# First three bands interleaved, first step without conv3, VectorE's order changed in the last steps

## The chip, the cores and the metric

The kernel runs on one core of one Trainium2 chip. The metric is the device time of one execution in microseconds (us), as the median over several executions. The core's engines run side by side and meet only at semaphores: TensorE (PE, its weight loads PEld), VectorE (DVE), ScalarE (ACT), GpSimd (POOL) and SyncE (SP), which issues the DMAs.

## The reference

For an image batch x of 8 x 128 x 128 positions with 64 channels, in float32:

```
q = x @ Q_P;  k, v = (3x3 neighbourhood of x) @ K_P, V_P
alpha = softmax(k . q * mask)           # over the 9 neighbours
t = x + sum(alpha * v)
u = relu(conv3x3(t, ff1) + b1)          # 64 -> 64    conv1
w = relu(conv3x3(u, ff2) + b2)          # 64 -> 128   conv2
out = t + relu(conv3x3(w, ff3) + b3)    # 128 -> 64   conv3
```

## The kernel before

The eight images are taken as four pairs; one image of a pair lies on partitions 0 to 63 (LOWER), the other on 64 to 127 (UPPER). An image is cut into 16 bands of 8 rows, so there are 64 bands. The bands run through the convolutions in one pipeline of steps, one band a step, with one draining step at the end of all.

**Attention of a band b.** `r_product` (L396) multiplies the band's x (tiles `xc` and `xs`) with `qk` = Q K^T; ACT copies the result to `rq` (`keep_r`). `masks` and `scores` (L409, L416) give the scores of patches of 8 x 8 positions against their 100 keys, in two halves; DVE takes the maxima (`max_scores`), ACT the exponentials (`exps`, 16 of them in four groups), DVE divides (`scale`). `turn` (L428) transposes the weights on PE and ACT copies them to `probt` (`keep_turned`). `mix` (L436) multiplies them with the keys' x (tile `xk`), ACT copies to `y` (`keep_y`), `v_product` (L447) multiplies with V, and DVE adds x (`add_x`, tile `xr`), which gives t in `tf`. `t_inputs` makes the inputs of conv1 (`dt`) of it. The attention of band b+2 is spread over the step of band b.

**The convolutions** are computed in Winograd form over the columns, each with four streams of products. DVE forms the inputs (`transform`, L879: part 0 the two middle streams, part 1 the two outer ones) and combines the results (`middle`, `outer`); ACT copies one bank (`keep_m2`, `keep_u2`) and applies bias and relu. Conv1 is `wholes` and `quarters` (L468, L477), conv3 four tiles of `conv3_tile` (L484), conv2 `begin2`, `go_on2`, `end2` (L532 to L564) for four tiles j. Conv3 of a step works on what conv2 of the step before left, so in the first step of all it has nothing real to work on, and its result is not stored. Conv3's first tile waits for `middle1` of the first image, its third for `outer1` and part 1 of the inputs.

**Before the first step** the attention of bands 0, 1 and 2 runs one after the other (L580 to L604 on PE, L795 on ACT, L986 on DVE): PE does all that belongs to a band before the next band begins. DVE prepares the weights of conv1 after the attention of band 0 and those of conv2 (`split_weights`) after that of band 1; GpSimd prepares those of conv3. SP issues nine small constants first, then the loads of band 0 and the weights; bands 1 and 2 are loaded into the same tiles as band 0 once its scores are done. PE waits for all weights before the first step.

**The steps.** `schedule` (L204) runs `step` on each engine: one first step, then per pair a first, fourteen middle and a last one. The last four steps of the last pair have the kinds ASK (all of the attention), MIX (only the rest from `mix` on), V (only from `v_product` on) and 0 (none); a draining step and four last tiles of conv3 follow. Each engine follows the order written out in its own `step`. DVE's (L1002) begins with `outer` of conv2 of the step before, `add_x`, `inputs` ODD part 0, ODD part 1, EVEN part 0, and `middle1` of both images.

Of the kernel before, what the change touches and what calls it, by code (L numbers as in the profile page):

```python
# [15 lines left out]
BAND = 8  # L16
# [15 lines left out]
FINAL = RUN + 1  # L32
DRAIN, LAST = BANDS, BANDS + 1
# [46 lines left out]
def build(nc, x_bands, x_keys, qt2, kt, vbd, w1, w2, w3, b1, b2, b3, window, eye, eye16, out):  # L80
    with ExitStack() as ctx:
# [27 lines left out]
        xk = sb("xk", [KEYS, PATCHES, 128], F32)  # L109
        xr = sb("xr", [128, RP, 2, W], F32)  # L110
# [22 lines left out]
        deven = sb("deven", [128, RP + 1, 4, 2, WT], F32)  # L133
        d_new = {CONV1: du, ODD: dodd[:, 2:RP + 2], EVEN: deven[:, 1:RP + 1]}
# [13 lines left out]
        r_banks = conv_banks[:, 2:4]  # L148
# [12 lines left out]
        w_ready = sem("w_ready")  # L161
# [6 lines left out]
        xr_in = sem("xr_in")  # L168
        r_done = [sem(f"r{i}_done") for i in range(2)]
# [79 lines left out]
        def split_weights(engine, wait, raw, wh, wl, mid, half, stage):  # L249
# [7 lines left out]
            engine.tensor_scalar(g2, g2, -1.0, None, ALU.mult).then_inc(stage, 1)  # L257
            wait(stage, 3)
            streams = ((0, g0), (1, mid[:, 0]), (2, mid[:, 1]), (3, g2))
            for m, g in streams:  # L260
                last = engine.tensor_copy(wh[:, m], g)
            last.then_inc(stage, 1)
            wait(stage, 4)
            for m, g in streams:
                last = engine.tensor_tensor(wl[:, m], g, wh[:, m].bitcast(F32), ALU.subtract)
# [14 lines left out]
        def _(sp):  # L280
            for dst, src in ((qt_sb, qt2), (kt_sb, kt), (v_sb, vbd), (window_sb, window), (eye_sb, eye),
                             (eye16_sb, eye16)):
                sp.dma_start(dst[:], src).then_inc(const_in, 16)
            for i, src in enumerate((b1, b2, b3)):
                sp.dma_start(bias[:, i:i + 1], src).then_inc(const_in, 16)

            def load_xc(b):
                sp.dma_start(xc[:], x_bands[b]).then_inc(xc_in, 16)

            def load_xs(b):  # L290
# [3 lines left out]
            def load_xk(b):  # L294
                sp.dma_start(xk[:], x_keys[b]).then_inc(xk_in, 16)
# [35 lines left out]
            keep_first(1, 0)  # L331
            sp.wait_ge(scores_done, 24)
            load_xs(3)
            load_xc(3)
# [14 lines left out]
            def step(G, p, k, b, par, att):  # L349
                if att >= V:  # L350
                    sp.wait_ge(t_ready, b * 2 + 2)
# [33 lines left out]
            sp.wait_ge(xk_in, 16 * LOADS)  # L385
            sp.wait_ge(xs_in, 32 * LOADS)
            sp.wait_ge(xr_in, 64 * LOADS)
            sp.wait_ge(xc_in, 16 * LOADS)

        @block.tensor  # L390
        def _(pe):
            def await_r(b):
                pe.wait_ge(xc_in, b * 16 + 16)
                pe.wait_ge(xs_in, b * 32 + 32)

            def r_product(b):  # L396
# [19 lines left out]
            def scores(b, half):  # L416
# [19 lines left out]
            def mix(b, half):  # L436
                if half == 0:
                    pe.wait_ge(xk_in, b * 16 + 16)
                pe.wait_ge(probt_ready, b * 2 + (half + 1))
                for a in range(HALF):  # L440
                    patch = half * HALF + a
                    for i, image in enumerate((LOWER, UPPER)):
                        last = nc.tensor.matmul(far_banks[image, half, a * C:(a + 1) * C], xk[:, patch, image],  # L443
# [3 lines left out]
            def v_product(b):  # L447
                moving = y[:].rearrange("c a (r s) -> c a r s", s=PATCH)
                for odd in range(2):
                    for i, image in ((1, UPPER), (0, LOWER)):  # L450
                        to = UPPER if odd != i else LOWER
                        bank = near_banks[to, i].rearrange("c (a r s) -> c a r s", r=RP, s=PATCH)
# [79 lines left out]
            def begin2(G, k, j, b, att):  # L532
# [7 lines left out]
                elif j == 2:  # L540
                    if att == ASK:
                        pe.wait_ge(probt_ready, b * 2 + 6)
                    elif att:
                        pe.wait_ge(t_ready, b * 2 + 2)
# [30 lines left out]
            pe.wait_ge(const_in, 16 * 9)  # L575
# [4 lines left out]
            for b in range(3):  # L580
                if b:
                    await_r(b)
                    pe.wait_ge(r_ready, b * 2)
# [563 lines left out]
```

## Time and profile before

| what | value |
| --- | --- |
| median of 3 executions | 2083.73 us (2083.67 to 2085.44) |
| profiled execution | 2084.2 us |
| its span in the profile | 2082.4 us |
| PE, DVE, ACT, POOL busy | 97%, 87%, 52%, 1% of the span |
| mean granted clock of PE | 0.992 |
| DMA | 320.89 MB, mean 154 GB/s |

The span is what the profiler saw from the first to the last instruction; the profiled execution took 1.8 us more than it. The granted clock is a share of PE's full 2.4 GHz: 1.00 or, when it is halved, 0.50; a stretch that holds both shows a value between. Matmul ends are modelled, so an overlap of a row with the next is no contradiction.

### The profile page before, as it was taken

The numbers are of one execution on the slowest core, as the hardware profiler recorded it, in microseconds if no ns is written. First come the engines' busy times: TensorE is split into PE (matmuls) and PEld (weight loads), VectorE is DVE, ScalarE is ACT, GpSimd is POOL, SyncE is SP. The second block draws the span as 40 slices with busy tenths as digits, with TensorE's granted clock in tenths as the row PEclk, the third lists the DMA queues.
The fourth block names the chain that finished last, engine by engine and source line by source line (L and its number), as shares of the span: only waits on it lengthen the run. The fifth ranks groups of instructions, "written<-read, shape, count | busy, mean of one in ns | idle before, by whom it ended". The sixth has DMA issues, their size and how long they took to land.

```text
span 2082.4 us, 61988 instructions
## 1 busy us (share of the span) xinstructions
PE 2025.3 (97%) x23866; PEld 1240.9 (60%) x23866; DVE 1815.4 (87%) x2502; ACT 1088.4 (52%) x3086; POOL 17.2 (1%) x28
## 2 busy tenths in 40 slices
PE   4899999999999999999999999999999999999997
PEld 3566656656665655655656655665656665665554
DVE  3699899899899899899889899899888989989986
ACT  3464555555555555555555455455455455455422
POOL 3000000000000000000000000000000000000000
PEclk9899999999999999999999999999999999999999
DMA  5555555555555555555555554554555555554532
GB/s 146 124 149 170 164 143 171 156 148 167 155 152 167 155 157 158 157 163 150 160 158 155 161 168 141 165 167 140 166 165 141 170 162 144 168 166 144 155 128 86
DMA packets 286054, 320.89 MB, mean 154 GB/s; under 512 B 87802, under 2 KB 220218, under 8 KB 279482
## 3 DMA queue, kind: packets, MB, share of 16 engines
q1 hardware_dynamic: 285982, 319.92, 53.0%
q8 instruction: 46, 0.75, 0.2%
q14 instruction: 26, 0.21, 0.0%
HBM read 150.23 MB, written 33.82 MB: 88 GB/s over the span
## 4 chain that ended last, share of the span: by engine, by line
PE 96%; DVE 2%; ACT 1%; issue 1%; DMA 0%; SPq 0%; DVEq 0%; ACTq 0%
PE conv_banks L502 32%; PE conv_banks L462 16%; PE conv_banks L527 13%; PE side_banks L527 13%; PE side_banks L443 6%; PE side_banks L422 4%; PE conv_banks L402 4%; PE side_banks L431 3%; PE side_banks L453 3%; PE side_banks L414 2%; ACT prob L724 1%; DMA xs<-x_bands 0%; DVE work L962 0%; DVE deven L882 0%; DVE deven L883 0%
## 5 line engine op out<-in xcount | busy, mean ns | idle before, releaser
L502 PE MATMUL conv_banks<-dodd,w3f 128*64 128x512 f32 (+2 forms) x1616 | 491.4, 581 | 11.0 <-DVE work L929 9.3
L502 PE MATMUL conv_banks<-deven,w3f 128*64 128x512 f32 (+2 forms) x1616 | 490.3, 579 | 0.0
L724 ACT ACTIVATE prob<-side_banks,negmax 128x100 f32<-128x100 f32 x1024 | 344.9, 378 | 162.5 <-DVE negmax L847 162.5
L462 PE MATMUL conv_banks<-dt,w1f 128*64 128x256 f32 (+2 forms) x4128 | 377.6, 378 | 0.0
L462 PEld LDWEIGHTS conv_banks<-dt,w1f 128*64 128x64 f32 (+1 forms) x4128 | 233.7, 135 | 121.0 <-issue 42.1
L502 PEld LDWEIGHTS conv_banks<-dodd,w3f 128*64 128x64 f32 x1616 | 148.3, 137 | 245.4 <-issue 219.7
L724 ACT ACTIVATION_READ_ACCUMULATOR prob<-side_banks,negmax 128x1 f32 x1024 | 246.9, 241 | 0.0
L502 PEld LDWEIGHTS conv_banks<-deven,w3f 128*64 128x64 f32 x1616 | 152.8, 137 | 143.1 <-issue 139.7
L736 ACT COPY rq<-conv_banks 128x512 f32<-128x512 f32 x128 | 68.7, 589 | 305.2 <-PE conv_banks L402 305.2
L962 DVE TENSOR_TENSOR work<-side_banks,work 128x1024 f32<-128x1024 f32 (+1 forms) x130 | 154.4, 1230 | 78.6 <-PE side_banks L527 78.6
L741 ACT COPY probt<-side_banks 100x1024 f32<-100x1024 f32 x128 | 130.2, 1017 | 157.2 <-PE side_banks L431 157.2
L527 PE MATMUL conv_banks<-duh,w2h 64*128 64x512 f32 (+2 forms) x788 | 166.6, 415 | 0.6 <-DVE work L953 0.6
L762 ACT COPY m_sb<-conv_banks 128x512 f32<-128x512 f32 x196 | 109.4, 593 | 104.6 <-PE conv_banks L527 100.3
L527 PE MATMUL side_banks<-duh,w2h 64*128 64x512 f32 (+2 forms) x788 | 157.6, 390 | 0.0
L901 DVE TENSOR_TENSOR dul<-work,duh 128x1024 fp32r<-128x1024 f32 (+1 forms) x130 | 156.7, 1205 | 0.0
L527 PE MATMUL side_banks<-duh,w2l 64*128 64x512 f32 (+2 forms) x788 | 156.5, 388 | 0.0
L443 PEld LDWEIGHTS side_banks<-probt,xk 100*64 100x64 f32 x4096 | 134.1, 141 | 36.2 <-issue 32.3
L527 PE MATMUL conv_banks<-duh,w2l 64*128 64x512 f32 (+2 forms) x788 | 155.3, 386 | 0.0
L783 ACT ACTIVATE relued<-work,bias 128x1024 f32<-128x1024 f32 (+1 forms) x130 | 142.2, 1145 | 23.2 <-DVE work L962 23.2
L953 DVE TENSOR_TENSOR work<-conv_banks,work 128x512 f32<-128x512 f32 x132 | 84.5, 683 | 76.7 <-PE conv_banks L502 76.6
L847 DVE TENSOR_REDUCE negmax<-side_banks 128x8 f32<-128x800 f32 x128 | 125.6, 982 | 19.8 <-PE side_banks L422 19.8
L791 ACT CAST duh<-work 128x1024 fp32r<-128x1024 f32 (+1 forms) x130 | 139.1, 1071 | 3.0 <-DVE work L883 2.8
(92 smaller groups left out, 3282.5 us busy)
## 6 DMA issues: line engine op xcount, KB each, us to landing
xk<-x_keys SPq DMA_DIRECT2D x65, 800.0 KB
xc<-x_bands SPq DMA_DIRECT2D x65, 650.0 KB, 4.8
xr<-x_bands SPq DMA_DIRECT2D x260, 128.0 KB, 2.9
dodd<-dodd SPq DMA_DIRECT2D x65, 512.0 KB, 5.6
out<-work SPq DMA_DIRECT2D x64, 512.0 KB, 4.1
xs<-x_bands SPq DMA_DIRECT2D x130, 128.0 KB, 3.1
dt<-dt SPq DMA_DIRECT2D x65, 256.0 KB, 4.8
deven<-deven SPq DMA_DIRECT2D x65, 256.0 KB, 6.1
```

Source lines behind the costliest of these rows:

```text
L443: last = nc.tensor.matmul(far_banks[image, half, a * C:(a + 1) * C], xk[:, patch, image], probt[:, half, i if a < GROUP else 1 - i, a], st ...
L462: mm = nc.tensor.matmul(bank[(LOWER, UPPER)[o], n * 256 + lo * 64:n * 256 + hi * 64], w1f[i][rows, m, s, o * C:o * C + C], dt[rows, lo + s ...
L502: mm = nc.tensor.matmul(bank[rows, lo_ * 128:hi_ * 128], w3f[:, m, s, odd * C:odd * C + C], source[:, lo_ + s // 2:hi_ + s // 2, m], start ...
L527: mm = nc.tensor.matmul(conv2_bank(which, j)[:, lo * 128:hi * 128], w[rows, STREAMS[j], 2 * (which == EVEN) + s], d[rows, lo + s:hi + s, S ...
L724: last = nc.scalar.activation(prob[:, g, a], score_banks[g // 2][:, g % 2, a * KEYS:(a + 1) * KEYS], ACT.Exp, bias=negmax[:, g, a:a + 1], ...
L741: nc.scalar.copy(probt[:, half], score_banks[half][0:KEYS].rearrange("n i (a q) -> n i a q", q=C)).then_inc(probt_ready, 1)
L762: nc.scalar.copy(m2_sb[:, which % 2, lo:hi], bank[:, lo:hi]).then_inc(act_read, 1)
L783: nc.scalar.activation(to[:, lo:hi, :, 1:1 + W], sums[which][:, lo:hi], ACT.Relu, bias=bias[:, 1:2]).then_inc(relu_done, 1)
L791: nc.scalar.copy(duh[:, 1:n + 1, streams], du[:, 0:n, streams]).then_inc(du_high, 1)
L847: nc.vector.tensor_reduce(negmax[:, 2 * half:2 * half + 2], score_banks[half][:, :, 0:GROUP * KEYS].rearrange("q g (a n) -> q g a n", n=KEYS),
L901: nc.vector.tensor_tensor(dul[:, 1:n + 1, streams], du[:, 0:n, streams], duh[:, 1:n + 1, streams].bitcast(F32), ALU.subtract).then_inc(du_ ...
L962: nc.vector.tensor_tensor(both, m03, both, ALU.add).then_inc(dve_read, 1)
```

## The change

Constants are issued by ACT's queue instead of SP's. Bands 1 and 2 get places of their own in `deven` and `dodd`, and the first band's keys a new tile `first_xk`, so that SP issues their loads early. The attention of the three bands is interleaved. `mix` and `v_product` of band 0 and `mix` of band 1 use two banks of `conv_banks`. The weights' one semaphore becomes three, and conv2's weights are prepared in two parts. The first step gets an order of its own on PE, ACT and DVE, without conv3's tiles on PE (DVE and ACT still treat conv3's banks); part of band 2's attention lies in it. In the steps after the last ASK step, DVE does part 0 of both inputs and `middle1` first. `add_x` treats both images in one call and signals once, so waits for `t_ready` count one per band.

```diff
@@ SP: constants leave, loads put forward
-            for dst, src in ((qt_sb, qt2), (kt_sb, kt), (v_sb, vbd), (window_sb, window), (eye_sb, eye),
-                             (eye16_sb, eye16)):
-                sp.dma_start(dst[:], src).then_inc(const_in, 16)
...
-            load_xk(0)
+            load_xk(0, first_xk, first_xk_in)
+            sp.wait_ge(pool_zeroed, 1)
+            load_xs(1, xs_of[1], early_in[0])
+            load_xc(1, xc_of[1], early_in[0])
+            load_xr(0)
+            load_xs(2, xs_of[2], early_in[1])
+            load_xc(2, xc_of[2], early_in[1])
+            load_xk(1)
             sp.dma_start(raws[2], w2).then_inc(w2_in, 16)
-            load_xr(0)
             sp.dma_start(raws[3], w3).then_inc(w3_in, 16)
-            for b in range(2):
-                sp.wait_ge(scores_done, b * 8 + 8)
-                load_xs(b + 1)
-                load_xc(b + 1)
-                sp.wait_ge(mixed, b * 2 + 2)
-                load_xk(b + 1)
-            sp.wait_ge(t_ready, 2)
+            sp.wait_ge(scores_done, 8)
+            load_xs(3)
+            load_xc(3)
+            sp.wait_ge(t_ready, 1)
             load_xr(1)
             keep_first(1, 0)
-            sp.wait_ge(scores_done, 24)
-            load_xs(3)
-            load_xc(3)
+            sp.wait_ge(mixed, 4)
+            load_xk(2)
@@ PE: the three bands
+            r_product(0)
+            pe.wait_ge(const_in, 16 * 7)
+            pe.wait_ge(r_ready, 2)
+            masked_scores(0)
+            pe.wait_ge(early_in[0], 48)
+            r_product(1, xc_of[1], xs_of[1])
+            turns(0)
+            pe.wait_ge(first_xk_in, 16)
+            mix(FIRST, 0, first_banks, first_xk)
+            mix(FIRST, 1, first_banks, first_xk)
+            pe.wait_ge(probt_ready, 2)
+            pe.wait_ge(r_ready, 4)
+            masked_scores(1)
+            pe.wait_ge(y_ready, 2)
+            v_product(0, first_banks)
+            pe.wait_ge(early_in[1], 48)
+            r_product(2, xc_of[2], xs_of[2])
+            turns(1)
+            pe.wait_ge(probt_ready, 4)
+            pe.wait_ge(r_ready, 6)
+            masked_scores(2)
+            pe.wait_ge(t_ready, 1)
+            mix(1, 0, first_banks)
+            mix(1, 1, first_banks)
+            pe.wait_ge(w1_ready, 1)
             pe.wait_ge(dt_done, 2)
+            pe.wait_ge(y_ready, 4)
             await_r(3)
@@ PE: the first step
+            def first_step(b):
+                G, k = FIRST, 0
+                r_product(b + 2)
+                wholes(k, False, True)
+                quarters(k, False, False)
+                pe.wait_ge(r_ready, b * 2 + 6)
+                wholes(k, True, True)
+                quarters(k, True, False)
+                pe.wait_ge(w2_ready, 1)
+                for _ in range(4):
+                    pe.sem_inc(tile_done)
+                turns(2)
+                pe.wait_ge(probt_ready, 6)
+                values_and_scores(b, ASK)
+                for j in range(2):
+                    begin2(G, k, j, b, ASK)
+                    go_on2(G, k, j)
+                for j in range(2):
+                    end2(G, k, j)
+                pe.wait_ge(exp_done, b * GROUPS + (2 * GROUPS + 2))
+                mix(b + 1, 0)
+                mix(b + 1, 1)
+                pe.wait_ge(y_ready, b * 2 + 4)
+                turns(b + 2)
+                for j in (2, 3):
+                    begin2(G, k, j, b, ASK)
+                    go_on2(G, k, j)
+                pe.wait_ge(w3_ready, 1)
+                end2(G, k, 2)
+                end2(G, k, 3, lambda: await_next(G, b, ASK))
@@ ACT: before the steps (keep_* in halves), and the first step
+            halves(keep_r, 0)
+            attend(0)
+            halves(keep_r, 1)
+            halves(keep_turned, 0)
+            halves(keep_y, 0, first_banks)
+            attend(1)
+            halves(keep_r, 2)
+            halves(keep_turned, 1)
+            exps(2, 0)
+            exps(2, 1)
+            halves(keep_y, 1, first_banks)
+            halves(keep_r, 3)
+            exps(2, 2)
+            exps(2, 3)
...
+                keep_u2(G, k, 0)
+                keep_u2(G, k, 1)
+                halves(keep_turned, b + 1)
+                relu_conv1(G, k)
+                keep_m2(G, k, CONV3)
+                u_high(G, k, 0)
+                attend(b + 2)
+                halves(keep_y, b + 1)
+                u_high(G, k, 1)
+                halves(keep_turned, b + 2)
+                keep_m2(G, k, ODD)
+                keep_m2(G, k, EVEN)
@@ DVE: before the steps, the first step, the last steps
+            maxima(0)
             dve.wait_ge(w1_in, 48)
+            whole_weights(nc.vector, dve.wait_ge, raws[0], w1f[0], half1[:, 0], w1_stage[0])
+            scalings(0)
+            whole_weights(nc.vector, dve.wait_ge, raws[1], w1f[1], half1[:, 1], w1_stage[1]).then_inc(w1_ready, 1)
+            maxima(1)
             dve.wait_ge(pool_zeroed, 1)
+            add_x(None, 0, 0, first_banks)
             for part in range(2):
                 t_inputs(None, 0, 0, part)
+            scalings(1)
+            dve.wait_ge(w2_in, 16)
+            combine_weights(nc.vector, dve.wait_ge, raws[2], w2_mid, half2, w2_stage)
+            maxima(2)
+            split_weights(nc.vector, dve.wait_ge, raws[2], w2h, w2l, w2_mid, w2_stage).then_inc(w2_ready, 1)
+            scalings(2)
...
+                middle1(G, k, 0)
+                middle1(G, k, 1)
+                outer1(G, k)
+                dve.wait_ge(w3_ready, 1)
+                inputs(G, k, CONV1, 0)
+                add_x(k, b, par)
+                maxima(b + 2)
+                inputs(G, k, CONV1, 1)
+                middle(G, k, CONV3)
+                outer3(G, k)
+                u_low(G, k, 0)
+                finish(G, k, b)
+                scalings(b + 2)
+                t_inputs(G, b, par, 0)
+                t_inputs(G, b, par, 1)
+                u_low(G, k, 1)
+                middle(G, k, ODD)
+                middle(G, k, EVEN)
...
+                else:
+                    inputs(G, None, ODD, 0, 1)
+                    inputs(G, None, EVEN, 0, 1)
+                    middle1(G, k, 0)
+                    middle1(G, k, 1)
+                    if att:
+                        add_x(k, b, par)
+                    inputs(G, None, ODD, 1, 1)
```

## Rows read from the trace of the kernel before

**Rows 1.** the page, busy time of the engines, share of the span and instructions.
```profile
PE 2025.3 (97%) x23866; PEld 1240.9 (60%) x23866; DVE 1815.4 (87%) x2502; ACT 1088.4 (52%) x3086; POOL 17.2 (1%) x28
```

**Rows 2.** windows: stretch, length, busy PE PEld DVE ACT POOL, granted clock, DMA share, GB/s.
```profile
69.35:103.08 33.73, 33.00 (x380) 20.24 (x380) 21.14 (x30) 14.95 (x46) 0.00 (x0) 0.94 0.44 116
...
1933.71:1964.51 30.80, 30.80 (x370) 18.86 (x368) 27.93 (x38) 16.90 (x48) 0.00 (x0) 1.00 0.54 159
```

**Rows 3.** timeline of SP and PE, from 0 us: start, duration, what, idle before and releaser.
```profile
0.73 0.59 SPq L283 DMA_DIRECT2D qt_sb<-qt  x1
...
5.46 0.43 SPq L288 DMA_DIRECT2D xc<-x_bands  x1
...
5.94 1.33 SPq L292 DMA_DIRECT2D xs<-x_bands  x2
...
12.36 1.12 PE L402 MATMUL conv_banks<-xc,qk 64*64 64x512 f32 x2 [4.58 <-DMA xs<-x_bands]
```

**Rows 4.** windows, 10 to 15 us (last value GB/s); and POOL's timeline.
```profile
10.00:15.00 5.00, 2.32 (x12) 0.56 (x12) 0.00 (x0) 0.55 (x1) 0.00 (x0) 1.00 1.04 227
...
29.04 1.30 POOL L270 TENSOR_TENSOR work<-work 128x512 f32<-128x512 f32 x1 [20.16 <-DMA work<-w]
```

**Rows 5.** timeline of PE, 30 to 75 us, one row of each kind of attention work.
```profile
32.40 1.99 PE L453 MATMUL side_banks<-y,v_sb 64*64 64x512 f32 x8 [0.68 <-ACT y L731]
...
47.78 1.09 PE L431 MATMUL side_banks<-eye_sb,prob 64*100 64x64 f32 x16 [1.51 <-DVE prob L858]
...
50.00 3.68 PE L443 MATMUL side_banks<-probt,xk 100*64 100x64 f32 x64 [1.13 <-ACT probt L741]
...
57.11 1.61 PE L422 MATMUL side_banks<-xc,rq 64*64 64x100 f32 x32 [0.33 <-ACT rq L736]
...
69.35 1.12 PE L402 MATMUL conv_banks<-xc,qk 64*64 64x512 f32 x2 [1.73 <-DVE dt L887]
```

**Rows 6.** timeline of DVE and of ACT, 18 to 55 us.
```profile
18.14 0.99 DVE L847 TENSOR_REDUCE negmax<-side_banks 128x8 f32<-128x800 f32 x1 [10.09 <-PE side_banks L422]
...
24.76 0.99 DVE L858 TENSOR_TENSOR prob<-prob,expinv 128x800 f32<-128x800 f32 x1
...
47.64 0.69 DVE L251 TENSOR_TENSOR work<-work 128x512 f32<-128x512 f32 x1
...
54.03 0.69 DVE L265 TENSOR_TENSOR w2l<-work,w2h 128x512 fp32r<-128x512 f32 x1
...
24.36 1.03 ACT L741 COPY probt<-side_banks 100x1024 f32<-100x1024 f32 x1
```

**Rows 7.** chain of waits, 10 to 70 us: start, duration, engine, line.
```profile
59.89 5.33 ACT prob L724 x32
```

**Rows 8.** timeline of PE and DVE, 71 to 104 us, the first step.
```profile
71.27 3.92 PE L462 MATMUL conv_banks<-dt,w1f 128*64 128x256 f32 x32
...
78.61 2.76 PE L462 MATMUL conv_banks<-dt,w1f 128*64 128x256 f32 x32
...
98.66 0.56 PE L527 MATMUL side_banks<-duh,w2h 64*128 64x512 f32 x2
...
103.08 0.71 PE L402 MATMUL conv_banks<-xc,qk 64*64 64x512 f32 x2
...
94.94 1.21 DVE L901 TENSOR_TENSOR dul<-work,duh 128x1024 fp32r<-128x1024 f32 x1
```

**Rows 9.** timeline of PE and DVE from 1964 us, and a window.
```profile
1972.75 1.50 PE L502 MATMUL conv_banks<-dodd,w3f 128*64 128x512 f32 x5 [1.20 <-DVE work L929]
...
2028.46 1.50 PE L502 MATMUL conv_banks<-dodd,w3f 128*64 128x512 f32 x5 [1.36 <-DVE work L929]
...
2054.07 2.82 PE L502 MATMUL conv_banks<-dodd,w3f 128*64 128x512 f32 x5 [4.46 <-DVE work L929]
...
2051.33 1.22 DVE L887 TENSOR_TENSOR dodd<-relued 128x1024 f32<-128x1024 f32 x1
...
2050.00:2054.00 4.00, 0.00 (x0) 0.00 (x0) 3.92 (x9) 1.43 (x4) 0.00 (x0) 0.92 0.23 89
```

More of the change, by code:

```diff
@@ L133, in build @@
         deven = sb("deven", [128, RP + 1, 4, 2, WT], F32)
+        xc_of, xs_of = [xc], [xs]
+        for t, lo in ((deven, 1), (dodd, 2)):
+            flat = t[:, lo:lo + RP].rearrange("c s m i w -> c (s m i w)")
+            xc_of.append(flat[:, 0:HALO * WP].rearrange("c (r w) -> c r w", w=WP))
+            xs_of.append(flat[:, HALO * WP:HALO * WP + BAND * W // 2].rearrange("c (r w) -> c r w", w=W // 2))
         d_new = {CONV1: du, ODD: dodd[:, 2:RP + 2], EVEN: deven[:, 1:RP + 1]}
@@ L414, in masks, with scores @@
                         nc.tensor.matmul(banks[half][n][to], eye16_sb[rows, rows], mask[rows], start=True, stop=False)
-            def scores(b, half):
+            def scores(b, half, xc=xc):
                 for a in range(GROUP):
@@ L434, in turn, with mix @@
                             last.then_inc(turned, 1)
-            def mix(b, half):
-                if half == 0:
-                    pe.wait_ge(xk_in, b * 16 + 16)
+            def mix(b, half, banks=far_banks, xk=xk):
+                if half == 0 and b is not FIRST:
+                    pe.wait_ge(xk_in, b * 16)
                 pe.wait_ge(probt_ready, b * 2 + (half + 1))
@@ L579, in _, with masked_scores, turns @@
             pe.wait_ge(xs_in, 32)
[L580 to L583, printed above, removed]
-                    pe.sem_inc(phase_begun)
-                r_product(b)
-                if b:
-                    pe.wait_ge(probt_ready, b * 2)
-                    pe.sem_inc(phase_begun)
-                masks(0)
-                pe.wait_ge(r_ready, b * 2 + 1)
-                scores(b, 0)
-                masks(1)
-                pe.wait_ge(r_ready, b * 2 + 2)
-                scores(b, 1)
+            def masked_scores(b):
+                for half in range(2):
+                    masks(half)
+                    scores(b, half, xc_of[b])
+            def turns(b):
                 for half in range(2):
@@ L706, in pair @@
                     step(g0 + h + 2, 2, g0 + h + 3, ASK)
-            step(0, 0, 1, ASK)
+            first_step(1)
             for p in range(PAIRS - 1):
@@ L810, in step @@
                     keep_r(b + 2, 1)
-                if p is not None:
-                    relu_conv2(G, None, ODD, 1)
-                    relu_conv2(G, None, EVEN, 1)
+                relu_conv2(G, None, ODD, 1)
+                relu_conv2(G, None, EVEN, 1)
                 keep_u2(G, k, 0)
@@ L978, in _ @@
             nc.vector.tensor_copy(qk[:], near_banks[:, 0, 0:C]).then_inc(qk_ready, 1)
-            def attend(b):
-                for half in range(2):
-                    max_scores(b, half)
-                for half in range(2):
-                    scale(b, half)
-            attend(0)
-            dve.wait_ge(w1_in, 48)
-            for i in range(2):
-                last = whole_weights(nc.vector, dve.wait_ge, raws[i], w1f[i], half1[:, i], w1_stage[i])
-            last.then_inc(w_ready, 1)
@@ L991, in _, with maxima, scalings @@
-            add_x(None, 0, 0, 1)
-            add_x(None, 0, 0, 0)
-            attend(1)
-            dve.wait_ge(w2_in, 16)
+            def maxima(b):
+                max_scores(b, 0)
+                max_scores(b, 1)
+            def scalings(b):
+                scale(b, 0)
+                scale(b, 1)
+            maxima(0)
+            dve.wait_ge(w1_in, 48)
+            whole_weights(nc.vector, dve.wait_ge, raws[0], w1f[0], half1[:, 0], w1_stage[0])
+            scalings(0)
+            whole_weights(nc.vector, dve.wait_ge, raws[1], w1f[1], half1[:, 1], w1_stage[1]).then_inc(w1_ready, 1)
@@ L1010, in step @@
+            def step(G, p, k, b, par, att):
+                if p is None:
+                    return first_step(G, k, b, par)
+                outer(G, None, ODD, 1)
+                outer(G, None, EVEN, 1)
+                if att == ASK:
+                    add_x(k, b, par)
                     inputs(G, None, ODD, 0, 1)
@@ L1019, in step @@
                     max_scores(b + 2, 1)
-                if p is not None:
-                    inputs(G, None, EVEN, 1, 1)
+                inputs(G, None, EVEN, 1, 1)
                 inputs(G, k, CONV1, 0)
```

136 lines of the change are left out of this document (65 added, 71 removed).

## The prediction

> **What bounds the kernel.** I read the page's busy shares first: PE works 97% of the span, DVE 87% [rows 1]. The windows say where. A repeating step is 30.80 us and PE is busy for all of it, DVE for 27.93 [rows 2]. The change touches none of these 60 or so steps' work, so it can only gain at the ends. There the timelines show the room. Before the first step PE works in short pieces, each behind DVE, ACT or a load [rows 3, 5]; the first step begins at 69.35 and the second at 103.08 [rows 5, 8]. In the last four steps PE waits for DVE ahead of conv3, 1.20 to 4.46 us [rows 9]. I sum against the profiled execution, whose span is 2082.4 us and whose time is 2084.2, 0.47 above the median of 2083.73.
>
> **Part 1: the constants leave SP's queue.** Nine issues lie between 0.73 and 5.46 [rows 3]. Band 0's loads then start 4.73 us earlier. Their last piece was issued near 6.6 and landed at 12.36, so r_product(0) starts near 7.6. ACT now issues the nine (some 5 us by the same rows) while it has nothing else to do, and its first copy, on data that is ready anyway, draws the table load off the path.
>
> **Part 2: the loads.** While its queue is full the DMA moves 227 GB/s [rows 4]. The order is now (MB): band 0 0.91, conv1's weights 0.77, first keys 0.80, band 1 0.91, xr 0.51, band 2 0.91, keys of band 1 0.80, conv2's weights 0.77, conv3's weights 0.77. Before, conv3's weights, 4.5 MB down the queue, were in at 29.04 [rows 4]; with 0.2 MB of constants, bytes from about 7.2 us on and 227 GB/s they would have come at 27.9, and some loads issued later are served among them, so I add 0.7 MB to each place. From 2.5 us on that gives: band 1 at 20 to 22 (at 18 without the addition), xr at 24, band 2 at 27.5, conv2's weights at 34.5. Only band 1 is on the path.
>
> **Part 3: the three bands.** Durations: r_product 1.92 (69.35 to the 71.27 at which conv1 begins) [rows 5, 8]; a band's scores in two halves with masks about 3.9 (two of 1.61 and what lies between) [rows 5]; maxima 0.99 a half, exponentials 5.33, scaling with its reciprocal 1.2 a half, transposes 1.09 a half, copies to probt 1.03 a half, mix 3.68, v_product 1.99 [rows 5 to 7]. These are PE's times at the half clock. Followed through the new order:
> - r_product(0) 7.6 to 9.6, copies to 10.8, scores(0) to 14.7, exponentials 14.1 to 19.4, with conv1's first weights on DVE beside them; last scaling to 20.7.
> - r_product(1) waits for band 1: 21.1 to 23.0. Transposes(0) to 25.3, mix(0) to 29.1, scores(1) to 33.0, v_product(0) to 35.0, r_product(2) to 37.0. This is where the interleaving pays: exponentials(1) run from 32.2 to 37.5 beside PE's work.
> - DVE: add_x(0) to 36.5, t_inputs(0) 2.4 to 38.9, scalings(1) to 40.1 and 41.3. Transposes(1) to 42.5, probt at 43.6, scores(2) to 47.6, mix(1) to 51.3, y copied: the first step would begin at 52.0. With PE at full clock for mix and scores it is 3 us less, by half of each of the last two pieces: 49.0.
> I take 50.5, for PE has no gap from 21 to 37 but one of 3 us at 37. Against 69.35 that is 18.9 us.
>
> **Part 4: the first step**, T its start. Conv3's four tiles on PE are gone, some 10 us of matmuls, but what the step then waits for is DVE and ACT, since they keep their share and take band 2's rest. PE: r_product to T+1.9, conv1's inner half 3.7 more to T+5.6, outer half 2.76 to T+8.3 [rows 8]; transposes(2) to T+9.6. ACT: exponentials(2,2..3) wait behind keep_r(3): T+3.0 to T+5.65; conv1 copies; probt to T+11.1; relu 1.2 to T+12.3. DVE: scaling(2,1) to T+6.9, middle1 1.4, outer1 1.2 to T+9.8, then inputs part 0 (after the relu) to T+13.6, add_x(1) to T+14.9, a maximum; PE's second half of scores(3) to T+16.0; maximum to T+17.1, inputs part 1 to T+18.3, middle 1.3 to T+19.6, outer3 1.2 to T+20.8, u_low 1.2 to T+22.0, finish to T+23.1, scalings(3) to T+25.4. PE: conv2's tiles 0 and 1 start at T+19.7, wait for u_low, end at T+25.4; mix(2) 1.9, y copied at T+28.0, transposes(3) to T+29.3, probt at T+31.2 (behind u_high(1) on ACT), conv2's tiles 2 and 3 take 4.4 (98.66 to 103.08 [rows 8]): T+35.6. Single DVE and ACT instructions of 1024 columns are 1.2 us [rows 8, 9]. So the first step is not shorter than its 33.73 [rows 2], it is 2 us longer; a chain of PE, ACT and DVE has taken the place of PE's own work. The second step begins at 50.5 + 35.6 = 86.1 against 103.08: 17.0 us.
>
> What is late next: on SP, load_xk(3) waits for mix(2) at T+27.3, and behind it in the queue stand the copies in dodd and deven and six of `kept`. Some 2.1 MB at 227 GB/s land near T+38; add_x(2), which waits for them, would run near T+39. Its cover is about 1 us. I put 0.3 on the sum; the bounds are 0 and 3.
>
> **Part 5: the last steps.** The new order takes inputs ODD part 1 (1.2 [rows 9], of which 1.13 until the next starts) and, in MIX and V, add_x (1.2) out from in front of middle1. In MIX and V that makes middle1 earlier than conv1's end, and the whole 1.20 goes, twice (the wait in V has the same value) [rows 9]. Step 0 and the draining step have no add_x: each gains the 1.13 of their 1.36 and 4.46. Together 4.7. Tile 2 of conv3, which needs what was moved back, comes 2.6 us after tile 0, and DVE reaches that point no later than before.
> In the draining step PE's granted clock falls to half in its wait: the window of 4 us shows 0.92, so it fell some 0.6 us before 2054, at about 2053.4 (0.08 of 4 us is 0.32, twice for the half), and five matmuls take 2.82 instead of 1.50 [rows 9]. Started at 2052.9, ahead of that point, they run at full clock: 1.3 more. I count it; without it the forecast is 1.3 higher.
>
> **Sum.** 17.0 - 0.3 + 4.7 + 1.3 = 22.7. The span becomes 2059.7, the profiled time 2061.5, the median 2061.0.
>
> A rule that speaks against the full clock: "HAM K=8/8 doesn't engage" for transposes, says the Trainium skill, TensorE: Matmul & The Clock Gate, Part 4: PE-mode transpose. The three sets of transposes before the first step would then not help to raise the clock. The rows cannot say: their 1.09 comes after waits on DVE, at half clock [rows 5]. It is the first rival.
>
> **Rivals.**
> - PE stays at the half clock before and in the first step. For: in the kernel before, its mix, scores and transposes near 47 to 58 us all have the slow times [rows 5]. Against: there PE idles for most of each band. T is 52.0, the step some 1 us longer (scores and v_product of the step): 17.0 falls to 14.5; with the tail's clock 2063.5, without 2064.8.
> - The loads come later, all sharing the DMA, so band 1 lands at 25 instead of 21 (its neighbours xr and band 2 are issued right behind it). T + 4, 2065. Against: what the queue moved before.
> - Band 1 at 18, full clock from the mix on: T near 47.5, 3 us less, 2058; the step itself could also lose 1 us at conv1's first half: 2057.
> - The change does not do what it says before the steps: band 2's rest, pushed into the first step, keeps PE waiting for as long as was won. That needs a first step of 52 us; my chain has 35.6 with its handoffs. Then only the tail's 4.7 to 6 are left, 2078.
> - Slower: first_xk shifts the places of all later tiles, and DVE's instructions in the repeating steps become slower by that. DVE has 30.80 - 27.93 = 2.87 us of room in each [rows 2]; beyond that PE waits. Over about 59 steps the 22.7 are used up at 0.39 us a step, so the point is DVE 3.3 us longer in each, 12%. At 0.5 us a step: 29.5 - 22.7, 2090.5. No row shows a place to matter.
>
> **How the numbers follow.** Forecast 0.48 (its own range 2059 to 2063); half clock 0.18; late loads 0.13; quicker 0.17; not as said 0.02; slower 0.02. Within 0.2% (4.2 us, about what a measurement tells from no change) of before lies nothing but a mix of the last two. So faster 0.97, same 0.01, slower 0.02. The range 2056 to 2067 takes in the forecast, both clock cases and the nearer part of the late loads.
>
> **What would show it.** Right: r_product(0) near 7.6; r_product(1) released by a load at 20 to 22; first step's conv1 near 52.5, second step's r_product near 86; in the first step PE waiting about 3.5 us ahead of conv2's first tile and 2 us ahead of its third; no wait ahead of conv3 in MIX and V, 0.2 in the step after, 3.3 in the draining step with matmuls at full rate behind it; repeating steps still 30.8. Wrong: a first step well above 36 us or the second stalled on `kept` would be Part 4; a start of the first step off 49 to 52 is Part 2 or 3; a repeating step that is not 30.8 would break the frame.

## The result, and the profile after

| | before | after |
|---|---|---|
| time, median (range) | 2084.53 us (2083.67 to 2085.44, 4 runs) | 2068.73 us (2068.25 to 2069.45, 4 runs) |
| profiled execution, span | 2082.4 | 2067.6 |
| first step begins | 69.35 | 53.62 (forecast 50.5) |
| second step begins | 103.08 | 93.11 (forecast 86.1) |
| first step | 33.73 | 39.49 (forecast 35.6) |
| repeating step, start to start | 31.0 | 31.0 |
| from MIX's start to the end | 117.9 | 113.2 (forecast 111.9) |

After over before is 0.9925, with an interval of 0.9909 to 0.9940: faster, by 15.8 us where 22.7 were forecast. 2068.73 lies above the range of 2056 to 2067. In the spans the gain is 14.8: 10.0 ahead of the second step and 4.7 in the last steps. Between the two only 0.1 moved. The missing 7.9 are 3.1 of a late first step, 3.9 of a longer one and 1.3 at the end, less the 0.3 put on for `kept`, which weren't paid, and that 0.1. The prediction's 30.80 for a repeating step is the length of the last ASK step alone. The others are 31.0 from start to start in both kernels, except the second step and those around the change of a pair, so nothing in the sum depends on it.

The page's busy line of the kernel after, beside [rows 1]: PE has 48 matmuls fewer (conv3's four tiles of the first step), and GpSimd is busy for 3.2 us more with six instructions of the same kind.
```profile
PE 2014.8 (97%) x23818; PEld 1237.0 (60%) x23818; DVE 1817.8 (88%) x2502; ACT 1088.2 (53%) x3087; POOL 20.4 (1%) x28
```
Windows of the kernel after: the first step; a repeating step; two stretches in which conv2 runs in the first step; the wait ahead of conv3 in the draining step, and the first microsecond behind it. The repeating step is 31.00 with PE busy for all of it, as before (133.30 to 164.30 there), and the first step's clock is 0.79, not 0.94.
```profile
53.62:93.11 39.49, 29.54 (x364) 21.62 (x364) 24.53 (x36) 19.15 (x64) 0.00 (x0) 0.79 0.42 107
123.34:154.34 31.00, 31.00 (x370) 18.81 (x368) 27.94 (x38) 16.93 (x48) 0.00 (x0) 1.00 0.55 162
74.00:79.00 5.00, 4.37 (x24) 3.88 (x26) 4.86 (x8) 1.57 (x10) 0.00 (x0) 0.50 0.89 232
87.00:90.00 3.00, 2.72 (x16) 2.52 (x18) 2.25 (x4) 1.20 (x3) 0.00 (x0) 0.51 1.00 206
...
2035.60:2038.90 3.30, 0.01 (x2) 0.00 (x0) 3.22 (x8) 1.83 (x4) 0.00 (x0) 1.00 0.40 155
2039.00:2040.00 1.00, 1.00 (x4) 0.28 (x6) 1.00 (x3) 0.00 (x0) 0.00 (x0) 0.75 0.00 0
```

**Ahead of the first step.** Timeline of PE in the kernel after, beside [rows 3, 5]. Read the brackets, which give the wait ahead of a row and what ended it. Band 0's r_product is near its forecast (7.33 for 7.6). Band 1's is at the forecast time too (21.22), but it follows PE's own late work and not a load, as had been forecast. Between them stand 8.57 us that end with the load of a bias.
```profile
7.33 1.11 PE L414 MATMUL conv_banks<-xc,qk 64*64 64x512 f32 x2 [0.32 <-DVE qk L1064]
...
17.88 0.55 PE L426 MATMUL side_banks<-window_sb,eye_sb 64*64 64x400 bf16 x4 [8.57 <-DMA bias<-b]
...
21.22 1.58 PE L414 MATMUL conv_banks<-deven,qk 64*64 64x512 f32 x8
...
53.62 1.12 PE L414 MATMUL conv_banks<-xc,qk 64*64 64x512 f32 x2 [2.42 <-issue]
```
The chain of waits there, and the DMA issues of the first 20 us with KB each and median time to landing. Three biases of 0.5 KB are the last of nine issues. One of them takes 6.1 us to land, the other two 11.7 and 12.2. Before, issued by SP ahead of everything, each took 2.1. PE's one wait for the constants covers all seven of them, for masks that need two.
```profile
5.68 12.15 DMA bias<-b
...
17.88 0.55 PE side_banks L426 x4
```
```profile
bias<-b ACTq DMA_DIRECT2D x3, 0.5 KB, 11.7
```
Timelines of DVE and of GpSimd (POOL), 38 to 51 us. Beside [rows 6] a scaling takes 1.82, not 0.99, and the first piece of conv2's weights 1.75, not 0.69, as long as GpSimd makes conv3's weights, which were 9.0 us before, from 29.04 [rows 4] on, and are 12.19 now. The two maxima at 48.72 read PSUM and keep to the duration of [rows 6].
```profile
39.24 1.82 DVE L943 TENSOR_TENSOR prob<-prob,expinv 128x800 f32<-128x800 f32 x1
...
42.96 1.75 DVE L266 TENSOR_TENSOR work<-work 128x512 f32<-128x512 f32 x1
...
48.72 1.88 DVE L932 TENSOR_REDUCE negmax<-side_banks 128x8 f32<-128x800 f32 x2
```
```profile
38.06 2.16 POOL L286 TENSOR_TENSOR work<-work 128x512 f32<-128x512 f32 x1 [29.18 <-DMA work<-w]
...
47.05 3.20 POOL L293 TENSOR_SCALAR w3f<-w3f 128x1024 f32<-128x1024 f32 x1
```

**The first step.** Timeline of PE, beside [rows 8]. All of conv1 takes 7.46, which is 5.45 at the full clock (rows of e6 and e10); the two waits are near the forecast, 3.5 and 2.
```profile
55.53 7.46 PE L474 MATMUL conv_banks<-dt,w1f 128*64 128x256 f32 x64
...
74.19 0.80 PE L539 MATMUL conv_banks<-duh,w2h 64*128 64x512 f32 x2 [3.68 <-issue]
...
87.28 0.79 PE L539 MATMUL side_banks<-duh,w2h 64*128 64x512 f32 x2 [1.67 <-ACT probt L791]
...
93.11 0.71 PE L414 MATMUL conv_banks<-xc,qk 64*64 64x512 f32 x2
```
**The last steps.** PE again, beside [rows 9]: MIX's and V's conv3 start without a wait, the next after 0.25, the draining step's after 3.32. The waits are those forecast; the five matmuls after the last should have taken 1.50.
```profile
2014.46 1.50 PE L514 MATMUL conv_banks<-dodd,w3f 128*64 128x512 f32 x5 [0.25 <-DVE work L1015]
...
2038.94 2.30 PE L514 MATMUL conv_banks<-dodd,w3f 128*64 128x512 f32 x5 [3.32 <-DVE work L1015]
```

### The profile page after: what moved, and what is told of

Read it like the earlier page. It is cut to its first block, busy times and chain, and to the rows that moved or that the text cites. A ratio compares the mean times of both kernels' runs of the same rounds, so it can differ in the third digit from the quotient of the medians.

```text
span 2067.6 us, 61916 instructions
## 1 busy us (share of the span) xinstructions
PE 2014.8 (97%) x23818; PEld 1237.0 (60%) x23818; DVE 1817.8 (88%) x2502; ACT 1088.2 (53%) x3087; POOL 20.4 (1%) x28
## 4 chain that ended last, share of the span: by engine, by line
PE 96%; DVE 2%; ACT 1%; issue 1%; DMA 1%; ACTq 0%; DVEq 0%
PE conv_banks L514 32%; PE conv_banks L474 16%; PE conv_banks L539 13%; PE side_banks L539 13%; PE side_banks L455 6%; PE side_banks L434 4%; PE conv_banks L414 3%; PE side_banks L443 3%; PE side_banks L465 3%; PE side_banks L426 2%; DMA bias<-b 1%; PE conv_banks L455 0%; ACT prob L774 0%; DVE work L1048 0%; DVE prob L943 0%
## 5 line engine op out<-in xcount | busy, mean ns | idle before, releaser
L514 PE MATMUL conv_banks<-dodd,w3f 128*64 128x512 f32 (+1 forms) x1592 | 483.6, 580 | 6.4 <-DVE work L1015 4.7
L514 PE MATMUL conv_banks<-deven,w3f 128*64 128x512 f32 (+1 forms) x1592 | 483.5, 580 | 0.0
L455 PEld LDWEIGHTS side_banks<-probt,xk 100*64 100x64 f32 x3968 | 127.0, 138 | 33.3 <-issue 32.1
```

The lines of the kernel that those rows point to most:

```text
L455: last = nc.tensor.matmul(banks[image, half, a * C:(a + 1) * C], xk[:, patch, image], probt[:, half, i if a < GROUP else 1 - i, a], start= ...
L514: mm = nc.tensor.matmul(bank[rows, lo_ * 128:hi_ * 128], w3f[:, m, s, odd * C:odd * C + C], source[:, lo_ + s // 2:hi_ + s // 2, m], start ...
```

## The experiments

Each ran beside the kernel before; the medians of that in the three sets of runs are 2084.2, 2084.8 and 2084.7. Except for e5, which starts from the kernel before, the edits are to the kernel after. A single execution of these kernels can lie 2 to 6 us from another of the same (e1: 2062.2 to 2068.0), and each profile is one execution, so medians carry the verdicts and the profiles the mechanism.

Two things vary between profiles without any edit that bears on them. Ahead of the first step after, e4 and e6 have the same code, and the step begins at 53.62, 55.47 and 53.90; its conv1 takes 7.46 in after and 5.45 in e4 and e6. The last steps, from MIX's start, are the same code in all but the kernel before. They take 112.9 to 113.2 in after, e3, e5, e6, e8, e9 and e10, but 114.0 in e2 and e11, and 115.1 to 115.6 in e1, e4 and e7. In the five longer ones PE's clock falls to half a second time, behind the draining step's wait and some way from the end. A window of e1, and one of after at the same distance from MIX's start:
```profile
2054.70:2058.10 3.40, 2.76 (x14) 2.00 (x16) 2.11 (x6) 0.68 (x2) 0.00 (x0) 0.50 0.40 157
```
```profile
2058.19:2061.59 3.40, 3.40 (x34) 2.08 (x31) 1.48 (x5) 0.37 (x1) 0.00 (x0) 1.00 0.14 55
```
So a difference of 2 us between two single profiles shows nothing by itself.

| | median (range, n) | ratio to before | first, second step begin |
|---|---|---|---|
| e1, masks wait for their own two loads | 2066.52 (2062.18 to 2068.01, 4) | 0.9889 to 0.9922 | 49.98, 89.53 |
| e2, constants back on SP | 2069.49 (2065.21 to 2071.30, 4) | 0.9913 to 0.9946 | 50.71, 88.00 |
| e3, GpSimd after conv2's weights | 2065.09 (2064.97 to 2066.84, 4) | 0.9891 to 0.9924 | 50.55, 88.79 |
| e4, conv3 back in the first step | 2073.97 (2072.43 to 2076.82, 4) | 0.9929 to 0.9962 | 55.47, 95.91 |
| e5, only the last steps changed | 2080.41 (2078.01 to 2083.26, 10) | 0.9971 to 0.9990 | 70.08, 103.27 |
| e6, without conv3's share of DVE, ACT | 2065.25 (2061.76 to 2068.34, 5) | 0.9897 to 0.9924 | 53.90, 86.35 |
| e7, e1, e3 and e6 together | 2060.44 (2059.21 to 2062.45, 4) | 0.9869 to 0.9899 | 47.48, 84.06 |
| e8, e7 with PE's early waits filled | 2057.59 (2056.06 to 2057.80, 4) | 0.9858 to 0.9888 | 44.97, 79.67 |
| e9, e8 with the first step filled too | 2057.58 (2055.91 to 2058.87, 4) | 0.9853 to 0.9883 | 47.66, 81.45 |
| e10, only PE's waits filled | 2068.53 (2066.89 to 2069.66, 5) | 0.9909 to 0.9936 | 54.04, 90.87 |
| e11, e8 with GpSimd as in after | 2060.17 (2056.29 to 2061.89, 4) | 0.9865 to 0.9895 | 47.28, 82.30 |

**e1: is it the late bias?**
```diff
-pe.wait_ge(const_in, 16 * 7)
+pe.wait_ge(mask_in, 32)        # window and eye16 only
...
+pe.wait_ge(const_in, 16 * 5)   # after r_product(1)
```


> The changed kernel, but PE waits ahead of scores(0) only for the two constants that the masks read (window and eye16); the other five, the biases among them, it awaits ahead of the transposes of band 0. Theory (the constants on ACT's queue land late among SP's large loads, and the wait for the biases, until 17.88 us, held scores(0) by 7 us): scores(0) start near 10.6 us; then the load of band 1 at 21 us is the next to hold PE, the transposes of band 0 start near 23.2 instead of 25.8, and the first step begins about 3 us earlier: 2065.5 us. Rival (the late constants are covered anyway, since the first step's start is set by VectorE and ScalarE later on): 2068.7 us, unchanged.

2.2 us faster than after, and in the profile the first step begins 3.64 earlier. Timeline of PE: the scores run at 10.82, and now band 1 is what PE waits for; it lands where Part 2 had put it. The profile's second step begins 3.6 earlier too, but the span is only 1.5 shorter, because its last steps are among the long ones (115.1 for 113.2).
```profile
10.82 0.55 PE L427 MATMUL side_banks<-window_sb,eye_sb 64*64 64x400 bf16 x4 [1.28 <-ACT rq L788]
...
21.15 1.98 PE L415 MATMUL conv_banks<-deven,qk 64*64 64x512 f32 x8 [7.13 <-DMA deven<-x_bands]
```
**e2: what did moving the constants bring?** The nine issues go back to SP, ahead of the loads.
```diff
-act.dma_start(dst[:], src).then_inc(qk_in, 16)      # and the seven const_in
+sp.dma_start(dst[:], src).then_inc(qk_in, 16)       # ahead of load_xs(0)
```

> The changed kernel, but the nine constants are issued by SP ahead of everything, as in the kernel before. Theory (the move to ACT's queue wins 4.7 us of issue time for the loads and loses most of it to the late landing of the constants): constants are in at 7.1 us, r_product(0) at 12.4, scores(0) near 15.6 (now 17.9), but band 1 lands near 25.5 instead of 21; the first step begins 0 to 2 us later: 2069.7 us. Rival (loads were never on the path, only the constants): scores(0) 2.3 us earlier and the whole kernel with them, 2066.4 us.

As expected: 0.8 us from the kernel after, so the move won nothing that a time shows. The 4.7 us of issues come back, the wait for the bias goes. Its one profile (span 2063.4) is the fastest of its runs, which go from 2065.2 to 2071.3; there the first step begins 2.9 earlier than in after, so a single profile would have said that SP is the better place.

**e3: does GpSimd slow DVE?**
```diff
+pool.wait_ge(w2_ready, 1)
```


> The changed kernel, but GpSimd prepares conv3's weights only after VectorE has finished conv2's. Theory (the two engines slow each other: scalings of band 1 took 1.82 us instead of 0.99, conv2's first weight part 5.8 instead of 3.1, and so the maxima of band 2, which ScalarE's exponentials and y wait for, came late): these durations go back, the first step begins 2 to 2.5 us earlier: 2066.4 us. Rival (off the path, or only moved to later VectorE instructions): 2068.7 us; if conv3's weights come too late for the first step's inputs, above 2069 us.

3.6 us faster, as that theory said. Timeline of DVE, beside the rows of after above: the same instructions with GpSimd silent.
```profile
38.81 0.99 DVE L943 TENSOR_TENSOR prob<-prob,expinv 128x800 f32<-128x800 f32 x1
...
40.86 0.68 DVE L266 TENSOR_TENSOR work<-work 128x512 f32<-128x512 f32 x1
```
**e4: what did leaving out conv3 bring?** PE runs conv3's four tiles on zeros in the first step again.
```diff
-for _ in range(4):
-    pe.sem_inc(tile_done)
+pe.wait_ge(w3_ready, 1)
+for j in range(4):
+    conv3_tile(G, k, j)
```

> The changed kernel with conv3's four tiles back in the first step on PE, after scores(3) and ahead of conv2, as they stood before. They are 10.3 us of matmuls. Theory (PE waits 3.7 us there anyway, and then runs conv2 at the half clock, which the tiles would prevent; so leaving them out is worth only a part of them): 10.3 - 3.7 - 2 to 3 for the clock = 4 us longer, 2072.7 us. Rival 1 (all of it on the path): 2079 us. Rival 2 (the lost clock takes back everything): 2068.7 us.

Near the theory: 5.2 us slower than after, for some 10 us of matmuls. The windows say why it isn't 10. With them PE's clock is 1.00 in the first step. The step is only 1 us longer than after's 39.49, but that flatters it, for conv1, which comes ahead of the added tiles, happened to be 2.0 slower in after. Against e2 and e10, which have after's order in the step and whose conv1 takes 5.45 as here, it is 3.2 and 3.6 longer (40.44 for 37.29 and 36.83). Another 2.1 are a stall in the second step, on DVE's add_x, which waits for a copy into `kept`: the thing that Part 4 named as late next. Of such a stall e10 pays 0.85 and e2 nothing, so e4 is 4.9 and 5.3 longer in all. The kernel after just escapes the stall. There the copies are issued from 85.56 on, 7.5 us ahead of the second step, and here from 89.67 on, 6.2 ahead.
```profile
55.47:95.91 40.44, 33.19 (x412) 20.42 (x412) 24.54 (x36) 18.99 (x64) 0.00 (x0) 1.00 0.39 97
```
```profile
101.27 1.29 DVE L955 TENSOR_TENSOR tf<-side_banks,xr 128x512 f32<-128x512 f32 x2 [2.75 <-DMA kept<-tf]
...
102.71 0.36 PE L426 MATMUL side_banks<-window_sb,eye_sb 64*64 64x400 bf16 x4 [2.12 <-DVE tf L955]
```
**e5: the last steps by themselves.** The kernel before, with DVE's order of the kernel after in its last steps.
```diff
+late = p is not None and att != ASK
-if att:
+if att and not late:
     add_x(k, b, par, 1)
...
-inputs(G, None, ODD, 1, 1)
+if not late:
+    inputs(G, None, ODD, 1, 1)
...
 middle1(G, k, 1)
+if late:
+    if att:
+        add_x(k, b, par, 1)
+        add_x(k, b, par, 0)
+    inputs(G, None, ODD, 1, 1)
```

> The kernel before with the change's order of VectorE in the steps after the last ASK step, and nothing else of the change. Theory (the last steps gave 4.7 us, as the two traces show from the MIX step to the end: 117.9 against 113.1): 4.7 us under the kernel before, 2079.5 us if that is 2084.2. Rival (the draining step's clock stays full when its wait is shorter, as I had counted): 6 us under it, 2078.2.

4.4 us (2.1 to 6.0): Part 5 without its clock term. The interval alone doesn't exclude the rival's 6; the profile does. From MIX's start to the end it has 113.1 for 117.9, the draining step's wait is 3.32, and the five matmuls behind it take 2.40, not 1.50.

**e6: the share of DVE and ACT.** In the first step PE's conv3 is gone in the kernel after, while ACT and DVE still read, add up and store its zeros. Here they don't.
```diff
-keep_m2(G, k, CONV3)                          # ACT
+act.sem_inc(act_read)
...
-middle(G, k, CONV3); outer3(G, k); finish(G, k, b)   # DVE
+dve.sem_inc(dve_read); dve.sem_inc(dve_read); dve.sem_inc(out_ready)
```


> The changed kernel, but ScalarE and VectorE leave conv3 out in the first step as PE does (its copy, middle, outer3 and finish; they only signal): 3.7 us less on VectorE between the inputs of conv1 and u_low. Their result was never stored, so nothing of the output changes. Theory (VectorE's chain sets the first step, not PE's work): conv2's first tile starts when the scores are done, 3.7 us earlier, u_low of part 0 is 2.5 us earlier, and the second step begins 2.5 us earlier: 2066.2 us. Rival (what binds is ScalarE's copies and PE's half clock behind them): 2068.5 us.

3.5 us faster. The profile shows 7.0 less in the first step, but 2.0 of them are conv1, which e6's edit doesn't touch (first row), and it is one of the faster runs. Timeline of PE: conv2 starts at T + 14.3 instead of T + 20.6 and then waits, 2.02 us, for the next thing that DVE owes it. The step is 32.45 us long at a clock of 0.95. That PE's clock stays up because it waits less for DVE fits these rows, but no run separates the two.
```profile
55.02 5.45 PE L474 MATMUL conv_banks<-dt,w1f 128*64 128x256 f32 x64
...
68.24 0.51 PE L539 MATMUL conv_banks<-duh,w2h 64*128 64x512 f32 x2 [0.26 <-issue]
...
71.42 0.73 PE L539 MATMUL conv_banks<-dul,w2h 64*128 64x128 f32 x5 [2.02 <-DVE dul L987]
```
**e7: do the three add up?** The edits of e1, e3 and e6 in one kernel.

> The changed kernel with three edits together: PE waits only for the masks' constants, GpSimd prepares conv3's weights after VectorE's, and ScalarE and VectorE leave conv3 out of the first step. Theory (three terms of one chain, each behind the other): 3 + 2.5 + 2.5 = 8 us less, 2060.7 us; the first step begins near 47.5. Rival (they cover one another, since the first step's start waits for one late event either way): about 4 us less, 2064.7 us.

8.3 us faster than after, from 2.2, 3.6 and 3.5 alone, which is 9.3 in all: they nearly do, and the rival's 4 is excluded. T is 47.48, and GpSimd's work, put off, now sits in the first step, where DVE waits 2.05 us for conv3's weights.
```profile
59.18 0.69 DVE L972 TENSOR_TENSOR work<-relued 128x512 f32<-128x512 f32 x1 [2.05 <-POOL w3f L294]
```
**e8, e10: is the half clock itself a cost?** Useless matmuls, whose results are overwritten, stand in PE's waits ahead of the first step.
```diff
+filler(first_banks, 5)      # e10: ahead of scores(0); in e8 36 mask matmuls
...
+pe.wait_ge(t_ready, 1)
+filler(first_banks, 2, xc_of[1], xs_of[1]); filler(r_banks, 1, xc_of[1], xs_of[1])
```


> The same three edits, and matmuls without use in PE's three longest waits before the first step (36 of the masks' kind after scores(0), 8 of r_product's kind after r_product(2), 4 after mix(1)); nothing reads their results. Theory (the shortfall behind the first step's start is PE's half clock, 20 us of which lie before and in the first step): the granted clock stays full from about 20 us on into the first step, and 2 to 3 us go: 2058.2 us. Rival 1 (the half clock is beside the path, which VectorE and ScalarE set): 2060.7 us, as without them. Rival 2 (they delay what waits behind them): 2062 us or more.

> The changed kernel with nothing but matmuls without use in PE's waits: 20 of r_product's kind in its wait for the constants, 8 after r_product(2), 4 after mix(1). Theory (of the shortfall, PE's half clock ahead of the first step and in conv1 is a part of its own): conv1 of the first step takes 5.45 us instead of 7.46, transposes, scores and mix of bands 1 and 2 run at full clock, and the second step begins 3 us earlier: 2065.5 us. Rival (the half clock lies beside the chain of VectorE and ScalarE): 2068.5 us.

On e7 they bring 2.9 us, as expected; on after alone 0.2 by the medians, nothing, where 3 were expected. In e10 the clock did rise (conv1 in 5.45, in the last row below), but PE ran into the same two things, the bias (released at 18.87) and DVE's probabilities beside GpSimd (a wait of 3.33): ahead of the first step the chain ran through these. Within the step the profile shows a gain, 36.83 for 39.49, but 2.0 of it are conv1's, which e6 got without filling, and nothing of it is left in the medians. So filling alone bought nothing that a time shows; with the two late things gone it bought 2.9. Windows of e8, and of e7 for its first stretch:
```profile
22.00:45.00 23.00, 17.93 (x388) 11.43 (x383) 16.36 (x28) 16.12 (x60) 0.00 (x0) 0.92 0.97 229
...
60.00:79.60 19.60, 15.93 (x180) 14.17 (x180) 11.71 (x15) 9.88 (x38) 0.00 (x0) 0.74 0.72 182
```
```profile
22.00:45.00 23.00, 15.89 (x320) 12.29 (x314) 13.35 (x22) 14.18 (x53) 0.00 (x0) 0.72 0.94 216
```
```profile
55.16 5.45 PE L474 MATMUL conv_banks<-dt,w1f 128*64 128x256 f32 x64
```
**e9: the same within the first step**, with a filler between the two halves of scores(3).
```diff
 scores(b + 2, 0)
+pe.wait_ge(dve_read, outer_read(G, CONV1))
+filler(first_banks, 2)
 pe.wait_ge(t_ready, b + 1)
```

> The kernel with the three edits and the filled waits, and 8 more matmuls without use in the first step, in PE's wait for add_x. Theory (conv2's first two tiles still run at half clock, after that wait): 1 to 1.5 us less, 2056.2 us. Rival (what is won in these tiles waits for u_low, or the clock falls in the next waits): 2057.6 us.

By the medians nothing more than e8. In the profile the step is 0.9 shorter (33.79 for e8's 34.71), and the second one loses 0.98 on `kept`'s copies. Conv2's first matmuls are at full rate (0.50 for two) and run into u_low, 2.01 us:
```profile
66.73 0.73 PE L540 MATMUL conv_banks<-dul,w2h 64*128 64x128 f32 x5 [2.01 <-DVE dul L1018]
```
**e11: GpSimd's place with the rest mended.**
```diff
-pool.wait_ge(w2_ready, 1)
```

> The kernel with the filled waits, but GpSimd prepares conv3's weights as soon as they are in, as in the changed kernel. Theory (it slows VectorE's scalings and weights by 2.5 us, but then isn't late for the first step's inputs, where VectorE waited for it some 1.2 us): 1.3 us more, 2058.9 us. Rival (the place of GpSimd's work is worth nothing net): 2057.6 us.

2.6 us slower than e8 by the medians, where 1.3 were expected. Its runs (2056.3 to 2061.9) overlap e8's, so 1.3 and 2.6 can't be told apart, nor is it shown that DVE is nearer the path here.

The best versions, e8 and e9, take 2057.6 us: 0.9873 of before (0.9858 to 0.9888), and 11.1 us less than the change as made.

## Why the prediction was wrong

The direction, the frame (only the ends move) and the mechanism of each part held. The sum was 7.9 too large, by these steps:

- **Part 1, constants leave SP's queue: the step that failed first.** It priced the nine issues and not their landings. "ACT issues the nine while it has nothing else to do" is right (0.73 to 6.1), r_product(0) starts at 7.33 (forecast 7.6), but their bytes now travel among SP's large loads: qt and kt landed in 4.8 and 5.0 us, the last biases in 12. scores(0) began at 17.88, not at 10.8. Shown by e1. The Trainium skill, DMA: Bandwidth & Descriptors, Issuing engines are not separate DMA queues, has it: transfers issued by different engines share the same DMA engines and interleave, so only issue time is saved. The trace agrees, and e2's times show the net: nothing clear of their spread.
- **Part 2, the loads: right.** Band 1 at 21.15 (e1's row; forecast 20 to 22).
- **Part 3, the three bands: one cost missing, one too large.** GpSimd's 9 us were given no place. They moved from 29.04 to 38.06, into DVE's scalings and conv2's weights, and two scalings and one piece of the weights alone ran 0.83, 0.84 and 1.06 longer. Shown by e3, and worth about 3 (3.6 by the medians). The Trainium skill, SBUF — State Buffer, Who interferes with whom, states that a DVE instruction with two SBUF inputs contends with a GpSimd instruction that reads SBUF. The trace agrees for these, and for the maxima, which read PSUM, it shows no slowing. With both costs gone T is 47.48 (e7), so the chain itself had been summed 3.0 too long; it hid half of the 6.1 left out. So it was luck that the 50.5 forecast for T was missed by 3.1 and not by 6. In the working the full clock for the last scores and mix was put at 3 us less; half of 3.9 and 3.7 is 3.8.
- **Part 4, the first step: the term that was mis-sized, 39.49 for 35.6.** Its chain of handoffs was right: conv1 began at T + 1.91 (forecast 1.9), the waits were 3.68 and 1.67 (3.5 and 2). PE's pieces were too short: conv1 7.46 for 6.46, so conv2 began at T + 20.6 for 19.7; tiles 0 and 1 7.55 for 5.7; tiles 2 and 3 5.83 for 4.4. Together they are 4.3 longer, and the handoffs between them took 0.4 back. I took these durations from a step in which PE is busy 33.00 of 33.73 us [rows 2] and put them into one in which I had myself counted idle time: PE was busy 29.54 of 39.49. The clock was 0.50 while most of conv2 ran; in e9, with conv2's first tiles at full rate, what follows u_low takes 3.5 (forecast 3.4), and in after 5.1. "PE stays at the half clock" had been priced at 1 us for the step, for scores and v_product alone. Conv1's 2.0 over the full rate belong to this one execution: in e6, with the same code, it takes 5.45. e4 is the other side: with conv3's matmuls back the clock is 1.00, and taking out 10 us of them is worth 5, of which 2 are the stall on `kept`. Filling one of PE's waits in the step won nothing that a time shows (e9); e6 did, by taking away what PE waits for.
- **What is late next: right, and the 0.3 were not needed.** The add_x that waits for `kept` wasn't delayed in after. PE pays 2.1 in e4, 0.85 in e10 and 0.98 in e9.
- **Part 5, the last steps: 4.7 for 4.7; the clock term, 1.3 more for 6.0 in all, failed.** In after, e1, e3, e5, e7 and e8 alike the draining step's wait is 3.32 or 3.33 and its five matmuls take 2.15 to 2.82. I had argued that matmuls started ahead of the fall run at full clock. But by the prediction's own figures the start at 2052.9 was only 0.5 us ahead of the fall at 2053.4, and the five need 1.50 us, so at most a third of them could have run ahead of it. In after they did start ahead of it: the clock is 1.00 through the whole wait and 0.75 in the microsecond behind it, so it fell in mid-work and was at half for the rest of the five. In e1 and e7 it had fallen already, and all five took the slow time.

Of the rivals, "PE stays at the half clock" came nearest, for the step rather than for the start. The transposes' rule couldn't be told from the idle time in any run. That the bands' loads share the DMA was the second rival; it was the constants that were late instead, while band 1 landed at 21. What stays open is the size of each term in a single execution: the clock's low stretches fall differently from run to run, and the 3.1, 3.9 and 1.3 come from one. The first of them stands against a start of the first step that varies by 1.85 with the same code (after, e4, e6), the second holds conv1's 2.0. Also open is how much of e2's equality with after is GpSimd's later start there.

## What to carry to other kernels

When a part of a kernel is emptied of PE's work, its remaining matmuls are not priced from the full kernel's rows: price them at the half clock first where PE waits between them, and ask what the removed matmuls covered. Here 5 of 10 us were won. Issuing small loads from a second engine saves the issue time alone; what waits for them must wait only for those it reads, and the biases' 12 us speak against issuing the smallest last (no run changes the order alone). And for each engine that is moved in time, even an idle one, ask whose instructions now lie beside it.

## What the runs showed of the hardware

- Two loads of 0.5 KB took 11.7 and 12.2 us from issue to landing, and a third 6.1, with the DMA engines filled from another issuer, and 2.1 with them nearly idle; those of 16 to 64 KB issued up to 5 us ahead of them took 4.5 to 6.5.
- Two-input DVE instructions on SBUF beside GpSimd: 1.82 for 0.99, 1.75 for 0.69; GpSimd's six instructions 12.19 for 9.0. Both sides pay. A DVE instruction with one SBUF input, the TENSOR_SCALAR on 128x512, took 1.25 beside GpSimd and 0.42 without (e3).
- Removing matmuls can lower the clock of those that are left: the step with 48 more, some 10 us of work, took 40.4 us at 1.00, those without 36.8 at 0.86 and 37.3 at 0.82 (e4 against e10 and e2, with the same conv1).
- The same code met the half clock in one execution and not in another: conv1 of the first step took 7.46 in after and 5.45 in e6, and the last steps took from 112.9 to 115.6.
- Filling PE's waits with useless matmuls raised the granted clock (0.72 to 0.92) and was worth 2.9 us on e7, and 0.2 on after, where a late load and DVE's scalings held PE ahead of the step.
